# Causal self attention of sixteen heads: probabilities made by keys instead of transposed

## What is computed

```
scores = einsum('bhqd,bhkd->bhqk', q, k) * scale        # scale = 16 ** -0.5
scores = where(causal, scores, -inf)
attn   = softmax(scores, axis=-1)
out    = einsum('bhqk,bhkd->bhqd', attn, v)
x      = layernorm(x + out @ Wo.T)      # D
x      = layernorm(x + out)             # E: q = x, k = v = ctx
```

## Time and profile before

| | |
|---|---|
| median of 3 runs | 764.21 us (762.01 to 766.28) |
| profiled execution, first to last instruction | 762.5 us |
| core, first score matmul to last router score | 293.66 to 538.13 us |
| TensorE busy | 670.0 us, 88% |
| VectorE busy | 555.0 us, 73% |
| ScalarE busy | 489.5 us, 64% |
| GpSimd busy | 249.2 us, 33% |
| TensorE's mean granted clock | 0.934 |

### The profile page before, as it was taken

One profiled execution on the slowest core, in us unless ns is written; L12 is line 12 of the kernel. 1 busy time (PEld: TensorE's weight loads), 2 busy tenths in 40 slices (PEclk: granted clock), 3 DMA queues, 4 the chain that ended last, 5 costly groups with the idle time before them and its releaser, 6 DMA issues.

```text
span 762.5 us, 18666 instructions
## 1 busy us (share of the span) xinstructions
PE 670.0 (88%) x4914; PEld 603.1 (79%) x4915; DVE 555.0 (73%) x2513; ACT 489.5 (64%) x1356; POOL 249.2 (33%) x420
## 2 busy tenths in 40 slices
PE   5889799858774888999999999999899979999982
PEld 5788578734443888999999999999899968888882
DVE  3788587767888546888898989998876735555474
ACT  4546566538772226999999999998555635555443
POOL 4343310133333700121212222222154625555651
PEclk9999899967885799999999999999999989999986
DMA  9960000000003387667776765661044423333175
GB/s 287 354 168 0 1 1 1 1 0 2 0 1 110 131 250 237 188 198 212 219 201 207 196 194 163 171 175 41 31 146 145 138 81 105 96 98 108 44 177 135
DMA packets 66488, 95.60 MB, mean 125 GB/s; under 512 B 11390, under 2 KB 52992, under 8 KB 66304
## 3 DMA queue, kind: packets, MB, share of 16 engines
q1 hardware_dynamic: 60912, 84.41, 38.0%
q0 software_dynamic: 5520, 10.53, 4.9%
HBM read 62.45 MB, written 33.36 MB: 126 GB/s over the span
## 4 chain that ended last, share of the span: by engine, by line
PE 39%; DVE 19%; issue 18%; DMA 11%; ACT 5%; POOL 4%; SPq 2%; DVEq 0%; POOLq 0%; ACTq 0%
PE bank L1955 9%; DMA xg<-X,idx 6%; PE bank L2106 6%; PE bank L1941 5%; PE bank L1687 4%; DVE bank L1406 3%; PE bank L2130 3%; PE bank L1930 3%; DVE smax L1406 2%; PE bank L2094 2%; PE bank L1971 2%; DMA late_mem<-yg 2%; DVE X L1151 1%; POOL rstd L625 1%; POOL xg L727 1%
## 5 line engine op out<-in xcount | busy, mean ns | idle before, releaser
L961 ACT ACTIVATE late_mem<-bank,smax 128x128 f32<-128x128 f32 x512 | 150.3, 409 | 15.3 <-DVE smax L1406 12.9
L1406 DVE CUSTOM_DVE_ANT_0 bank<-bank,causal 128x128 f32<-128x128 f32 x512 | 132.8, 322 | 17.7 <-issue 16.9
L1955 PE MATMUL bank<-f_mem,late_mem 128*128 128x68 f32 (+3 forms) x1024 | 127.8, 268 | 0.2
L1955 PEld LDWEIGHTS bank<-f_mem,late_mem 128*128 128x128 f32 x1024 | 124.6, 192 | 0.8 <-issue 0.5
L625 POOL TENSOR_TENSOR rstd<-var,power 128x2 f32<-128x2 f32 (+1 forms) x64 | 40.4, 632 | 189.7 <-DVE var L1144 178.2
L971 ACT ACTIVATE late_mem<-bank 128x512 f32<-128x512 f32 x128 | 82.6, 645 | 2.4 <-PE bank L1941 1.3
L1941 PE MATMUL bank<-ident,late_mem 128*128 128x128 f32 x512 | 78.4, 276 | 3.2 <-ACT late_mem L961 3.1
L1406 DVE DVE_READ_ACCUMULATOR2_ANT smax<- 128x1 f32 x512 | 71.8, 140 | 0.0
L1930 PE MATMUL bank<-kz,qs 128*128 128x256 f32 x256 | 63.8, 332 | 2.0 <-issue 0.9
L1941 PEld LDWEIGHTS bank<-ident,late_mem 128*128 128x128 f32 x512 | 59.2, 142 | 5.1 <-ACT late_mem L961 4.9
L2012 PE MATMUL bank<-x_hi,w_hi 128*128 128x256 f32 x176 | 51.0, 290 | 0.0
(11 more groups left out here) (285 smaller groups left out, 1991.8 us busy)
## 6 DMA issues: line engine op xcount, KB each, us to landing
qs<-q_D SPq DMA_DIRECT2D x64, 128.0 KB, 2.8
kz<-k_D SPq DMA_DIRECT2D x128, 64.0 KB, 2.6
qs<-q_E SPq DMA_DIRECT2D x64, 128.0 KB, 2.7
kz<-k_E SPq DMA_DIRECT2D x128, 64.0 KB, 2.5
xg<-f_mem SPq DMA_DIRECT2D x1, 5031.0 KB, 24.4
late_mem<-xg SPq DMA_DIRECT2D x39, 129.0 KB
q_D<-stage_d SPq DMA_DIRECT2D x8, 512.0 KB, 2.9
k_D<-stage_d SPq DMA_DIRECT2D x8, 512.0 KB, 3.9
```

Source lines behind the costliest of these rows:

```text
L961: ins = sc.activation(sp[:, g, i, :], bank[g][:, i * P:(i + 1) * P], ACT.Exp, bias=smax[:, g, i:i + 1], scale=-1.0)
L1406: ins = ve.tensor_tensor_reduce(v[:, i, :], v[:, i, :], causal[:, :], -1.0, 3e38, ALU.add, ALU.min, smax[:, g, i:i + 1])
L1955: ins = mm(bank[6][:, h * (DH + 1):to * (DH + 1)], spt[:, g, i, :], vf[:, slot, h:to, :].rearrange("p h d -> p (h d)"), start=True, stop=True)
```

## The change

The probabilities are made with keys on the partitions, so that they need no transposes.

- `scores` as before (96 contraction rows, three combinations of high and low parts instead of four), into two banks in turn instead of four. `maxima` is the old `softmax`; only `smax` is used of it.
- `xpose_max`: TensorE transposes the group's four columns of minus the maximum to four rows; ScalarE `shift_rows` writes them to contraction rows 96 to 99 of `qs`, where `kz` has a selector of ones for each head (`pick`, loaded once by `load_picks`).
- `shifted`: TensorE makes score minus maximum once more, with keys stationary and queries moving, one matmul of 128 columns for each head, 100 contraction rows. ScalarE `exps` takes one exponential of 128x512 without a bias. GpSimd `keep_past` sets what lies above the causal diagonal to zero.
- `values`: the values (16 columns, the ones and padding, 32 in all) are stationary, the probabilities move; the four heads of a group write to four different 32 partitions of bank 4. ScalarE `evac_o` copies the bank, TensorE `xpose_heads` transposes it back in four, `heads_out` divides as before.
- The normalising goes from VectorE to ScalarE (`apply_row`), with minus mean times inverse root from GpSimd (`row_scale`); `copy_row`, `keep_xt` and `xt1` go.
- `qs` and `kz` have three buffers instead of two, filled by 9 DMAs instead of 12; GpSimd zeroes them in three pieces, the third after the scatter target in HBM has been cleared.
- Lags grow by one turn or two (`TAIL` is 5), each engine's order is new, and `core_turns` writes every turn out instead of looping.

```diff
+def core_turns(stages, tail):
+    for s in range(2 * B + tail):
+        for lag, *steps in stages:
             if lag is None:
-                if s >= 2 * n:
-                    one(s - 2 * n)
+                if s >= 2 * B:
+                    steps[0](s - 2 * B)
                 continue
             t = s - lag
-            step, t = (one, t) if t < n else (two, t - n)
-            if step is not None and 0 <= t < n:
...
-WIDE = 4
-LAG_PT = 2
-LAG_PV = 4
-LAG_XP = 4
-LAG_XE = 3
+SLOTS = 3
+CELLS = 8
+DV = 32
+KS = 6 * DH
+KM = KS + HG
+LAG_MT = 2
+LAG_ST = 3
+TAIL = 5
...
-        xt1 = part(late_mem, 4096 + 2 * D, [P, 2, KC, P])
         ln0 = part(late_mem, 2048 + 3 * UT, [P, 2, UT])
-        qs = (rounded("qs0", "late_mem", 6400, [P, NP * P]), rounded("qs1", "f_mem", 3136, [P, NP * P]))
-        vf = part(f_mem, 4672, [P, 2, NH, DH + 1])
+        kz = (rounded("kz0", "late_mem", 4 * NH * P, [P, 2, NP * P]),
+              rounded("kz1", "late_mem", 4 * NH * P + 2 * NP * P, [P, 2, NP * P]),
+              rounded("kz2", "f_mem", 0, [P, 2, NP * P]))
+        qs = (rounded("qs0", "f_mem", 3136, [P, NP * P]), rounded("qs1", "late_mem", 6400, [P, NP * P]),
+              rounded("qs2", "late_mem", 5120, [P, NP * P]))
+        ot = part(late_mem, 7424, [P, NG * P])
+        vf = part(f_mem, 4672, [P, 2, NH, DV])
...
+            def load_stack(t):
+                phase, b, slot = "DE"[t // B], t % B, t % SLOTS
...
-                                  ).then_inc(sem(f"stack{slot}"), 16)
-                for c in range(4):
+                                  ).then_inc(sem(f"ld_set{slot}"), 16)
+                for c in range(3):
                     for h in range(2):
-                        sp_.dma_start(kz[c * 32 + h * DH:c * 32 + (h + 1) * DH, slot, h, :].bitcast(F32),
-                                      k_rows[c % 2, h * DH:(h + 1) * DH]).then_inc(sem(f"stack{slot}"), 16)
+                        sp_.dma_start(kz[slot][c * 32 + h * DH:c * 32 + (h + 1) * DH, h, :].bitcast(F32),
+                                      k_rows[c % 2, h * DH:(h + 1) * DH]).then_inc(sem(f"ld_set{slot}"), 16)
...
+            def load_picks():
+                for slot in range(SLOTS):
+                    for h in range(2):
+                        sp_.dma_start(kz[slot][KS:KM, h, :].bitcast(F32).rearrange("p (g n) -> p g n", g=NG),
+                                      sel[:, h, :].unsqueeze(1).to_broadcast([HG, NG, 2 * P])
+                                      ).then_inc(sem("selected"), 16)
...
+            sp_.wait_ge(sem("selected"), 16)
+            load_picks()
             for t in range(NU):
                 stage_unit(t)
                 if t == 1:
                     sp_.wait_ge(sem("staged0"), 32)
-                    load_stack("D", 0)
-                    load_stack("D", 1)
+                    load_stack(0)
...
+            sp_.wait_ge(sem("selected"), 16)
...
             pool.wait_ge(sem("C_o"), 2 * NU)
-            gp.memset(kz[:, :, :, :].bitcast(F32), 0.0).then_inc(sem("zeros"), 1)
+            pool.wait_ge(sem("ln_x"), LN["D"])
+            own.then(gp.memset(kz[0][:, :, :].bitcast(F32), 0.0))
+            own.then(gp.memset(kz[1][:, :, :].bitcast(F32), 0.0))
+            pool.wait_ge(sem("zeroed"), 16)
...
+            def keep_past(g):
+                def step(t):
+                    pool.wait_ge(sem("core_exp"), NG * t + g + 1)
+                    cell = pt[:, (NG * t + g) % CELLS, :, :]
+                    gp.affine_select(out=cell, in_=cell, compare_op=ALU.is_ge, fill=0.0, base=0,
+                                     pattern=[[0, HG], [1, P]], channel_multiplier=-1).then_inc(sem("core_pm"), 1)
                 return step
...
+            def row_scale(t):
+                slot = t % 2
+                inverse_root("D", 1)(t, slot)
...
+            stages = []
+            for g in range(NG):
+                stages.append(at(g, LAG_ST, keep_past))
+                if g == 0:
+                    stages += [(0, values(V), values(CTX))]
+                if g == 2:
+                    stages += [(4, row_scale, None), (3, None, row_scale)]
+            core_turns(stages, TAIL)
...
-            def exps(phase, g):
-                def step(t, slot):
-                    if not early(phase, t, 1):
-                        act.wait_ge(sem("core_pt"), NG * t + g - NG + 1 + before(phase, "pt"))
-                    act.wait_ge(sem("core_max"), NG * t + g + 1 + before(phase, "max"))
-                    for i in range(HG):
-                        ins = sc.activation(sp[:, g, i, :], bank[g][:, i * P:(i + 1) * P], ACT.Exp,
-                                            bias=smax[:, g, i:i + 1], scale=-1.0)
-                    ins.then_inc(sem("core_exp"), 1)
...
+            def shift_rows(g):
+                def step(t):
+                    n = NG * t + g
+                    act.wait_ge(sem("core_mt"), n + 1)
+                    cols = slice(g * 2 * P, (g + 1) * 2 * P)
+                    sc.activation(qs[t % SLOTS][KS:KM, cols].rearrange("p (i n) -> p i n", i=2),
+                                  bank[6][0:HG, D + n % 2 * P:D + (n % 2 + 1) * P].unsqueeze(1).to_broadcast([HG, 2, P]),
+                                  ACT.Copy).then_inc(sem("core_mr"), 1)
                 return step
-            def evac_pt(phase, g):
-                def step(t, slot):
-                    if not early(phase, t, 1):
-                        act.wait_ge(sem("core_pv"), NG * t + g - NG + 1 + before(phase, "pv"))
-                    act.wait_ge(sem("core_pt"), NG * t + g + 1 + before(phase, "pt"))
-                    sc.activation(spt[:, g, :, :], bank[4 + g % 2][:, :], ACT.Copy).then_inc(sem("core_pts"), 1)
+            def exps(g):
+                def step(t):
+                    n = NG * t + g
+                    wait_past(act, "core_pv", (n - CELLS) // NG + 1)
+                    act.wait_ge(sem("core_st"), n + 1)
+                    sc.activation(pt[:, n % CELLS, :, :], bank[2 + n % 2][:, :].rearrange("p (i n) -> p i n", i=HG), ACT.Exp
+                                  ).then_inc(sem("core_exp"), 1)
                 return step
...
+            def e_high(t):
+                act.wait_ge(sem("unit_xpose"), NU + t + 1)
...
+                    act.wait_ge(sem(f"staged{t % 2}"), 16 * NU + 16 * (t // 2))
+                sc.activation(stage_e[:, t % 2, 0, :], bank[4][:, 0:D], ACT.Copy, scale=float(DH) ** -0.5
                               ).then_inc(sem("D_hi"), 1)
...
-            stages = [(None, first_high, None)]
+            stages = [(None, first_high)]
             for g in range(NG):
-                stages += [both(g, LAG_PT, evac_pt), both(g, 0, exps)]
+                stages += [at(g, LAG_MT, shift_rows), at(g, LAG_ST, exps)]
                 if g == 0:
-                    stages += [(LAG_XP, e_high, None), (1, None, w_high)]
+                    stages += [(6, e_high, None), (5, apply_row, None), (4, None, apply_row)]
...
+                    stages += [(2, evac_o), (1, None, w_high)]
+                if g == 2:
+                    stages += [(3, evac_ot, None), (4, None, f_xt)]
+            stages.append((None, piece))
+            core_turns(stages, TAIL)
...
-            def softmax(phase, g):
-                def step(t, slot):
-                    dve.wait_ge(sem("core_s"), NG * t + g + 1 + before(phase, "s"))
-                    v = bank[g][:, :].rearrange("p (i n) -> p i n", i=HG)
+            def maxima(g):
+                def step(t):
+                    n = NG * t + g
+                    dve.wait_ge(sem("core_s"), n + 1)
+                    v = bank[n % 2][:, :].rearrange("p (i n) -> p i n", i=HG)
                     ve.memset(idle[:, 2 + g:3 + g], 0.0)
                     for i in range(HG):
                         ins = ve.tensor_tensor_reduce(v[:, i, :], v[:, i, :], causal[:, :], -1.0, 3e38,
...
+            def e_low(t):
+                slot = t % 2
                 dve.wait_ge(sem("D_hi"), 2 * NU + t + 1)
-                ve.scalar_tensor_tensor(stage_e[:, slot, 1, :], bank[NG - 1][:, 0:D], float(DH) ** -0.5,
+                ve.scalar_tensor_tensor(stage_e[:, slot, 1, :], bank[4][:, 0:D], float(DH) ** -0.5,
...
                     piece(k - 1)
-            pipelined_pair(dve, B, [(None, first_low, None), (LAG_XE + 1, None, f_scores), both(0, 0, softmax), (3, d_stats, None),
-                                    (2, None, e_stats), both(1, 0, softmax), (LAG_XP, e_low, None),
-                                    (3, d_apply, None), (2, None, e_apply), both(2, 0, softmax), both(3, 0, softmax),
-                                    (1, None, w_low), (1, heads_out("D"), heads_out("E")), (None, pieces, None)])
+            core_turns([(None, first_low), (5, None, f_scores), (6, e_low, None), (0, maxima(0)), (3, heads_out), (0, maxima(1)),
+                        (4, row_stats, None), (3, None, row_stats), (0, maxima(2)), (0, maxima(3)),
```

(76 more changed lines are left out.)

350 lines of the change are left out of this document (149 added, 201 removed).

## The result

The changed kernel takes 773.34 us (median of 20 runs, 764.38 to 781.17) where the kernel before took 766.18 (20 runs, 762.01 to 771.98): 1.0063 times as long, 95% interval 1.0041 to 1.0085. In a second comparison it was 1.0103 (1.0062 to 1.0144). So it is slower by 5 to 8 us, and I had forecast 762 and a small gain. Ratios go by the fast executions of both kernels and medians by all, and as the first profile is of the slowest of the 20, I show its rows where they say the same as the others and do the sums with a third profile (771.45 us, span 769.4).

What follows compares the result with a forecast made beforehand. TensorE, fullest of three nearly full engines, was taken to bound the core. Terms of -6.7, +2.1, +0.3 and +2.5 gave -1.8 on a 762.5 us span: 760.7, median about 762; range 745 to 806, own case 752 to 772.

Steps and rivals of the forecast that it cites:

- What bounds it now: Attention core before the change: three nearly full engines, TensorE the fullest, busy 98% at full clock; a D turn takes 7.49 us.
- The D cycle, 7.75: Layer D's turns: VectorE's low part waits for ScalarE, values wait for the low part; 7.75 us, VectorE idle about 1.1.
- second cycle (7.6): Layer D's turns: a loop through the maxima of group 2, on which the next scores wait; together 7.6 us.
- E, 6.8: Layer E's turns: VectorE's 6.45 and TensorE's 6.4 interlock, 6.8 us against 7.1 before; low end 6.5, high end 7.2.
- Value products, 1.8: TensorE, per turn: only one head's second record overlaps the next head's first, so 16 steps, 1.8 us.
- rival B: TensorE's values not side by side at all: 3.5 us a turn, total about 806, half-way some 783; chance 0.12, halves included.
- Shifted scores, 0.11 each: TensorE, per turn: 16 matmuls of 128 moving columns in rounded type, 0.11 us each, 1.76 in all.
- Rival A: TensorE's shifted scores cost 0.22 us each, total about 805; decides from 0.12 a matmul on; chance 0.15.
- Rival C: GpSimd's masks hold up VectorE's two-input instructions in layer E: turns 7.7 us, total about 774; chance 0.05.
- Ahead of the core nothing: Before the attention core: key-buffer fills, key splitting and selector loads fit into idle or waiting time, so cost nothing.
- The sum itself: Whole stage: turns 0 to 5 -6.7, 6 to 18 +2.1, 19 to 31 +0.3, tail +2.5; together -1.8 us.
- Tail, 14.7: From the last maximum to the last router score: 14.7 us against 12.2 before, +2.5.

Runs made afterwards that it cites:

- added work at two places: Changed kernel plus unread identity products on TensorE: eight before the core's waits, six in turn 0, eight in turn 19; 761.3 us, ratio 0.9909 to the kernel before.
- eight-product kernel: Changed kernel plus eight unread identity products on TensorE in turn 19's gap alone; 763.2 us, ratio 0.9961 to the kernel before.
- sixteen products: Changed kernel plus sixteen unread identity products on TensorE in turn 19's gap; 773.2 us, ratio 1.0077 to the kernel before.

## Why the prediction was wrong, step by step

- *What bounds it now*: held. *The D cycle, 7.75*: 7.83, with VectorE's stall and its releaser as named (1.61 where I had 1.1). Moving the low part in the queue gave 7.44, freeing the values of it as well 7.12. My second cycle (7.6) was no bound: 7.12 is below it.
- *E, 6.8*: 6.51 at full clock, my low end.
- *Value products, 1.8*: 1.08 with four side by side, near the low bound of 0.9. The rule that I chose, by which only the second record of one head lies beside the first of the next, is refuted by the 1.08; rival B is too. By the Trainium skill ("TensorE: Matmul & The Clock Gate", "Measured speedup vs the span model") three tiles give 2.38 times; the two orders here differ by 2.43 / 1.08 = 2.25 for four, the serial one already overlapped where strips change.
- *Shifted scores, 0.11 each*: four in 0.64, most of them 0.11 apart and some 0.14, 0.12 on the mean. Rival A's 0.22 is refuted, but its threshold of 0.12 was reached. *Selects, 0.9*: 0.64.
- *Rival C*: the hold-up is there, but small. E's sum of rows takes 0.62 with nothing of GpSimd beside it (it reads its rows in another order than before, when it took 0.42). When a select is under way it takes 0.76 to 1.00 and ends about 0.47 behind the select's end; four selects of the third profile that start 0.15 to 0.3 into such a sum take 1.05 instead of 0.64 and end 0.5 behind the sum. That is one standing still for the other, as the lock cited in the prediction has it. Mostly 0.15 us a turn meet this way, and E's turns stayed at 6.5.
- *Ahead of the core nothing*: wrong in the good direction, 6 to 8.4 us earlier in the three profiles, and no merit of the forecast. The traces put some 3.6 of the third profile's 7.5 down to VectorE's normalising, no longer beside GpSimd's fill, and the rest to SyncE's queue, which has 9 instead of 12 loads of each of the first two blocks ahead of the staged rows; neither is tested.
- *The sum itself* is the step that failed. It has no term for TensorE's granted clock. I took 2.4 GHz for granted since the earlier trace rows read 0.99 and 1.00, though 0.99 was the dip at the core's start, and though the change took away just what kept TensorE busy. I had even put the doubled statistic of turn 19 into the sum (1.3) without asking what TensorE would do meanwhile. The clock costs 9 to 11 us by the runs' means, of which added work at two places gave 8 to 11 back.
- *The same code runs as long as before*, which the sum takes as given: the second missing term, 4 us in a loop that the change doesn't touch. I had named waits for instructions as a sign of error, but looked for them in the core.
- *Tail, 14.7*: a term that was too small even at full clock, 18.0 (the eight-product kernel), and 20 to 21 in the changed kernel's profiles. The queue that I missed is ScalarE's: SiLU ahead of normalization.

At equal clock the change is worth some 3 us with the misplaced loop, some 7 without it, but these 7 are no larger than what was won ahead of the core, which nobody forecast. The core itself, put together from stretches at nearly full clock (turns 0 to 5 take 34.9 with products at both places; 6 to 18 take 102.1, 19 to 31 87.4 and the tail 18.0 with the eight in turn 19), would come out some 1.7 us shorter than before, and I had forecast 1.8. Part of that closeness is luck: turns 19 to 31 were 4 us better than forecast, the tail 3 us and turns 6 to 18 2 us worse.

What stays open: why the low stretches last longer in the changed kernel. At its start it has gaps of 0.94 and 0.96 us and then 10 to 14 us at 0.5; the kernel before has 0.94 and 1.90 there and 3.4. In the windows of 10 us above TensorE's records cover 98 to 100% of the time. Some low stretches of 3.4 us start with no gap over 0.6 us near (at 498.7 in the third profile, at 486.2 in that of eight products), so the gaps are not the whole rule. The Trainium skill ("TensorE: Matmul & The Clock Gate", Part 1) says that activity releases the throttle; the rows here show clock 0.50 beside 10.00 of 10.00 us busy, so busy time in the records alone does not tell when it is released. Whether the shape of the new products (4 and 32 columns of weights, 96 or 100 rows) has a part in it was not tried. Why sixteen products gave nothing in the median is open too. Nor is it known what in the loop's position makes its instructions late.

## What to carry to other kernels

Read the clock column before costing a change that relieves TensorE: here TensorE kept its clock through turns without gaps and lost it behind gaps of 1 to 2 us, and the price of a gap was the slow turns behind it, not its length. Fill or remove the gaps first (the place with two stalls in one turn, the start, the tail), then count instructions. If a loop that nobody touched gets slower by a constant part, compare its waits for issue and move its code. If one engine fills memory with zeros while another is on the critical path, look at whether the two slow each other: here that was 3.6 us. And a wait on a shared PSUM bank that stands at the head of a queue is worth a bank of its own: with the low part moved as well, that was 0.7 us in each of 13 turns, 0.3 of them the bank's.

## What the hardware showed beyond that

- Value products with 32 columns of weights, 32 records in four strips: 1.08 us side by side, 2.43 one strip after another.
- Rounded 4-byte products with 128 moving columns follow each other at 0.11 to 0.14 us, one record each; the added plain ones take two records of 0.11.
- The granted clock fell behind gaps of 1.9 to 2.1 us, in one run behind 1.19, and at the changed kernel's start behind two of 0.95, and then stood at 0.5 for 3.4 to 44 us; stretches of 3.4 us also came without a gap.
- GpSimd's select over 128x512 takes 0.64, and 1.05 when a VectorE sum of two SBUF rows began 0.15 to 0.3 us before it; that sum takes 0.62 alone and 0.76 to 1.00 when it begins behind a select or copy of GpSimd. Beside GpSimd's power of 128x1 (0.54 us) VectorE's two-input instructions took no longer (0.44).
- Two VectorE normalisings of 128x256 took 4.60 us beside a GpSimd fill of 128x4096 that took 3.51, and 0.74 without it.
